# Gated delta rule: the output projection of a quad moved behind the first products of the last merge level on TensorE

## What is computed

```python
q, k, v = conv_silu(x @ w_q), conv_silu(x @ w_k), conv_silu(x @ w_v)    # causal convolution of 4 taps
q, k = l2norm(q), l2norm(k)
def step(S, inp):                     # one token; S is a 64 x 128 state for each head
    q_t, k_t, v_t, g_t, b_t = inp
    S = S * exp(g_t)
    delta = (v_t - einsum('bhk,bhkv->bhv', k_t, S)) * b_t
    S = S + einsum('bhk,bhv->bhkv', k_t, delta)
    return S, einsum('bhk,bhkv->bhv', q_t * scale, S)
_, o = lax.scan(step, 0, (q, k, v, g, beta))
rms = o * rsqrt(mean(o * o) + EPS)
y = rms * norm_w * silu(x @ w_g)
return y.reshape(Bx, Tx, VDIM) @ w_out
```

## Time and profile before

| | us |
|---|---|
| median of 3 runs | 5018.24 |
| lowest and highest of them | 5017.36 and 5037.95 |
| the profiled execution, its own time | 5042.58 |
| its span, first to last instruction | 5040.4 |
| the gated delta rule's pipeline in that span | about 90 to 1360 |

### The profile page before, as it was taken

The page is one execution under the profiler, slowest core; times in us unless marked ns, Lnnn a source line. Parts: engine busy times, 40 slices in busy tenths (PEclk is TensorE's granted clock), DMA queues, the critical chain, the costliest instruction groups (busy, mean ns, idle before and its releaser), DMA issues. The chain is left out here.

```text
span 5040.4 us, 76528 instructions
## 1 busy us (share of the span) xinstructions
PE 4006.4 (79%) x20557; PEld 2446.3 (49%) x20557; DVE 3773.0 (75%) x6398; ACT 2416.6 (48%) x4996; POOL 2811.6 (56%) x2705
## 2 busy tenths in 40 slices
PE   5888888888578678577979955788888768888884
PEld 4666666666456456355447732233333323333332
DVE  5776777777467367456048866899999779999995
ACT  3555555555234234222236632566666436666661
POOL 2555555555344044043013330799999539999991
PEclk8998989999777778788999976899999879999997
DMA  1000000000000000000000000000000000000000
GB/s 49 8 9 9 8 9 8 9 8 8 16 0 0 21 0 0 12 0 24 0 17 1 1 15 8 0 0 0 0 0 0 8 0 0 0 0 0 0 0 13
DMA packets 90085, 33.33 MB, mean 7 GB/s; under 512 B 78032, under 2 KB 86112, under 8 KB 88928
## 3 DMA queue, kind: packets, MB, share of 16 engines
q1 hardware_dynamic: 89824, 30.16, 2.6%
HBM read 24.87 MB, written 5.24 MB: 6 GB/s over the span
## 5 line engine op out<-in xcount | busy, mean ns | idle before, releaser
L3023 POOL TENSOR_TENSOR dBx<-dtx,b_row 128x1024 f32<-128x1024 f32 x512 | 1220.2, 2383 | 3.9 <-ACT b_row L2989 3.9
L3057 DVE TENSOR_TENSOR_SCAN h<-banks,dBx 128x1024 f32<-128x1024 f32 x512 | 1167.7, 2281 | 18.2 <-ACT banks L2983 18.2
L2941 PE MATMUL banks<-hc,ident 128*128 128x512 f32 x2048 | 964.6, 593 | 0.0
L2983 ACT ACTIVATE banks<-dt,A 128x510 f32<-128x510 f32 x1024 | 661.6, 682 | 3.6 <-DVE h L3057 3.6
L2989 ACT ACTIVATE b_row<-banks 128x512 f32<-128x512 f32 x512 | 305.9, 598 | 573.8 <-PE banks L2925 573.8
L2941 PEld LDWEIGHTS banks<-hc,ident 128*128 128x128 f32 x2048 | 388.7, 190 | 272.0 <-issue 246.9
L3065 DVE TENSOR_TENSOR hc<-h,banks 128x768 f32<-128x768 f32 x512 | 477.8, 933 | 10.1 <-ACT c_row L2994 6.8
L3032 POOL TENSOR_TENSOR hc<-h,c_row 128x256 f32<-128x256 f32 x512 | 376.4, 735 | 53.7 <-ACT c_row L2994 29.0
L2925 PE MATMUL banks<-bc_lo,selectors 128*128 128x512 bf16 x1024 | 391.3, 382 | 0.0
L2924 PE MATMUL banks<-bc_hm_c,selectors 128*128 128x512 bf16 x512 | 197.3, 385 | 186.7 <-DVE hc L3065 186.4
L155 POOL MEMSET minus_half<- 128x16 f32 x13 | 1.5, 113 | 518.1 <-POOLq L234 180.3
(11 more groups left out here) (424 smaller groups left out, 9243.7 us busy)
## 6 DMA issues: line engine op xcount, KB each, us to landing
delta_blocks<-A_turned SPq DMA_DIRECT2D x256, 8.0 KB, 1.5
inv_turned<-delta_blocks SPq DMA_DIRECT2D x256, 8.0 KB, 1.7
blocks<-delta_blocks SPq DMA_DIRECT2D x32, 64.0 KB, 2.1
delta_blocks<-blocks_inv SPq DMA_DIRECT2D x32, 64.0 KB, 1.9
wh<-in_l1f_wh SPq DMA_DIRECT2D x1, 2048.0 KB, 8.2
wqkv<-in_l0f_wqkv SPq DMA_DIRECT2D x2, 768.0 KB, 4.3
residual<-in_x SPq DMA_DIRECT2D x1, 1024.0 KB, 4.8
wv<-in_l0a_wv SPq DMA_DIRECT2D x1, 1024.0 KB, 7.5
```

The source lines that it names most:

```text
L2941: i = nc.tensor.matmul(k.bank[e], k.ident[:], hc[:, s, e, :], start=False, stop=False)
L2983: i = nc.scalar.activation(a3[:, :, 1:], d3[:, :, 1:], ACT.Exp, scale=mem["A"][:, e, bass.ds(n, 1)])
L3023: nc.gpsimd.tensor_tensor(dBx[:, s % NS], dtx[:, :, bass.ds(c * SCH, SCH)], across(bsb[:, s % NS, :], SE), ALU.mult).then_inc(q["dbx_ready ...
L3057: v.tensor_tensor_scan(flat(h[:, s % NS]), flat(k.banks[:, at:at + SE, :]), flat(dBx[:, s]), 0.0, ALU.mult, ALU.add).then_inc(q["scanned"], 1)
```

## The change

In PE's `step`, the two calls of `merge_y` for level 6 go ahead of `out`. No instruction is added, removed or changed, on no engine, and the waits stay with their instructions.

```diff
                     if x0:
                         project(x0, 2)
+                    if x2:
+                        merge_y(x2, 2, 0)
+                        merge_y(x2, 2, 1)
                     if x3:
                         out(x0, x1, x3)
                     if x2:
-                        merge_y(x2, 2, 0)
-                        merge_y(x2, 2, 1)
                         merge_t(x2, 2, 0)
```

## The result

| | before | changed |
|---|---|---|
| median, us | 5020.76 (4 runs) | 5166.69 (4 runs) |
| lowest to highest | 5017.36 to 5037.95 | 5156.36 to 5173.57 |
| the profiled execution's own time | 5042.58 | 5173.57 |
| its span | 5040.4 | 5171.4 |
| mean granted clock over the span | 0.898 | 0.871 |

The changed kernel is **slower by 2.8%**: ratio 1.0276, 95% interval 1.0245 to 1.0306.

A forecast was written before the change was run, and what follows sets the result against it. PE was taken as fullest, each step's period closing through PE, then ACT and DVE. Full steps +8.4, less 1, plus 2.2 for draining steps gave +9.6 us on 5018.2, rounded to 5028 us; range 5003 to 5052.

The forecast's parts named there:

- the longer wait: PE behind wv: L1909 must wait for the transpose, so the first instruction starts 0.56 us later in each full step.
- the sign by which the forecast was to be known as wrong: Granted clock from 150 to 1290 leaving 0.92 by over 0.01, or no wait in front of L2412.
- L1931 without a wait: On PE, L1931 follows L2012 at once, its copy long done; it starts 0.24 to 0.34 us later than before.
- DVE's lead: DVE's next convolution starts 1.17 us earlier, but the norms wait for PE's sums of squares; gain costed at 0.
- The direct sum of +9.6 us: Full steps +8.4 us, less 1 for shifts lost at project(x0, 3), plus 2.2 for draining steps; chance 0.61.
- The bounds 5022 and 5036: Range of the forecast time in us from the lower and upper bounds on the delay of each full step.
- The draining steps: Two steps without an x0, where L2012 would now stand behind the transpose and L1909: +1.1 us each, +2.2 us.
- The step that failed: TensorE's clock: the longer pause and the broken run of small matmuls costed at nothing against each other.
- Rival A: Longer pause before L1909 brings slow clock into 15 full steps, +1.8 us each; 5055 us, chance 0.17.
- Rivals B and C: B: clock stays up, 5019 us (chance 0.13) or 4990 (0.05). C: DVE's gain arrives, 4994 us (0.04).
- C's condition: That the norms on DVE do not hang on PE's sums of squares, so 1.17 us a step comes off.

The follow-up runs named there:

- e2: Changed kernel plus two useless matmuls (512 and 256 columns) in PE's pause behind wv in the full steps; 5030.8 us, ratio 1.0009 to before.
- e5: Changed kernel plus one useless matmul of 256 columns in PE's pause behind wv; 5052.2 us, ratio 1.0039 to before.
- e3: Kernel before plus one useless matmul of 512 columns in its old pause ahead of L2012; 5035.0 us, ratio 1.0002 to before.
- e4: Changed kernel with DVE's transpose for T64 moved between the convolution's second and third tap; 5021.1 us, ratio 0.9973 to before.
- e8: e4 plus one useless matmul of 512 columns in the pause ahead of the level 4 products; 5011.8 us, ratio 0.9963 to before.
- e11: Kernel before plus one useless matmul of 512 columns in the pause ahead of the level 4 products; 5045.2 us, ratio 1.0026 to before.

## Why the prediction was wrong

**What held.** That both orders start behind the same convolution; the 0.15 us from the transpose to PE (0.15 in the step shown); the longer wait (47.0 us in 29 waits, 43 to 48 foretold); the sign by which the forecast was to be known as wrong, a clock that leaves 0.92 by over 0.01; L1931 without a wait; DVE's lead of about 1.2 us, which ends in a wait for the sums of squares and brings nothing. The direct sum of +9.6 us is consistent with e2, no more: its interval of 20 us is wider than the term. At the full clock, in e5, L1931 starts 2.97 us behind L1909 (712.65 against 709.68), and L1909 starts 0.61 behind the convolution's end (0.03, the transpose's 0.43 and 0.15), in sum 3.58. Before it was 3.36 from the convolution's end to L1931: +0.22, with 0.24 foretold for such a step. The bounds 5022 and 5036 were added up loosely: the terms give 5025 (5.5 - 1 + 2.2) and 5035 (16 - 1 + 2.2). Nothing hangs on it.

**The draining steps** were sized at +1.1 us each. From the transpose's start to L1931 it was 4.43 and is 6.16 in the changed kernel, +1.7:

```profile
1424.74 0.43 DVE L2402 STREAM_TRANSPOSE inv<-inv_turned 32x256 f32<-32x256 f32 x1 [2.88 <-ACT inv_turned L2153]
...
1425.32 1.94 PE L1909 MATMUL banks<-inv,A_turned 64*64 64x64 f32 x16 [1.21 <-DVE inv L2402]
...
1430.90 0.69 PE L1931 MATMUL banks<-inv_turned,steps 64*64 64x64 f32 x8
```

L1909 ran at the lower clock there, too.

**The step that failed** is the one on the clock: "I cost the two at nothing against each other and keep both as rivals." The sum went by durations at the higher clock, and the pause was one that the trace had never shown in this place in this length. What the runs showed in its place is 325 us more at the lower clock and about 122 us of time. Two arguments did not carry. "The present pause of 1.12 does not do it" is true (e3, and e5 at 1.14), but "the wait grows by only half of a us" was no comfort: the steep part lies between 1.14 and 1.62. And the gain set against it, L2012 parting the small matmuls from the sums of squares, was no counterweight: slow starts on L1848, L1955 and L1945 fell from 19 (68 us at the lower clock) to 13 (44 us), 24 us against 235 at the pause.

**Rival A's mechanism was borne out and its size was not.** It expected a step to go from 37.6 to 39.4 us, in 15 steps, 27 us; it was 4.6 us on average, in 28 of 29. The price was taken from a neighbour step with the clock at 0.91, that is 7 us at the lower level in 39.4. The changed kernel has about 8 us of it at the pause alone in each step, and about 6 more at level 4. The nearest row for the price was there: 3.51 for L1901 behind the turn of the loop, 1.5 us lost on a single group. The prediction put it behind "a pause of 2.54 us"; there is a second one of 1.86 between, and the slow stretch begins in that, so this row speaks of 4.4 us of idle in two parts. The six steps with the loop's turn took 42.3 to 45.6 us before, 5.6 to 8.9 more than the 36.7 of a step at the full clock. Their idle at the turn, from 150 to 1290, is

```profile
PE banks L1839 <- issue: 15.7, 6, 2.9
...
PE banks L1840 <- issue: 7.3, 6, 1.9
```

or 3.8 us a turn, which leaves 2 to 5 us. As an estimate, 29 x 5 = 145 us is what every step being hit could have cost, and the range should have reached there.

**Rivals B and C** did not come. C's condition was excluded by the rows, and DVE's 29 waits for L1848 show it. The Trainium skill's rule, that recent activity is what keeps the half-rate default away (page TensorE: Matmul & The Clock Gate, Part 1), was the one that spoke against the change. The trace agrees, with 0.80 in place of 0.92, and e2 with 0.93 shows it in the other direction.

## What to carry to other kernels

Before an instruction is moved ahead of another on TensorE, compare when each one's input is ready: behind the same producer, the one whose input comes second lengthens the pause by the whole difference, whatever it frees later. A pause of TensorE had a second price here, in clock, that was not in proportion to its length (no step hit at 1.14 us, 28 of 29 at 1.62). So a pause longer than the trace shows in that place needs a range that reaches to every step being hit. If the first of two waits can be met earlier on the other engine (e4), the same order turns into a gain, and where that can't be done, it may pay to fill the pause: a useless matmul of full size in it bought the clock back (e2).

## What the runs showed of the hardware that was not expected

A filling matmul of 256 columns, 0.43 us in a pause of 1.67, took away 311 us at the lower clock and 114 us of time (e5). What stood behind a pause counted as well: at 1.52 to 1.55 us of idle 10 of 37 steps were hit with full-size matmuls behind, 26 of 34 with 64-row ones. So did what the clock had just done: behind a slow stretch at level 4 every one of 38 steps was hit again. And stretches move: where one place is filled (e8, e11), more of them begin at another.
